# Scaling the softmax probabilities on GpSimd: the reciprocal as a broadcast tensor operand in place of a per-partition scalar

## What is computed

```python
xn = layernorm(x)
q, k, v = per-head projections of xn            # 16 heads, 64 wide, with biases
scores  = q @ k^T / sqrt(64), causal: -inf above the diagonal
att     = softmax(scores, axis=-1) / sqrt(64)
z       = att @ v
attn    = z.reshape(b, s, 16 * 64) @ proj
# feed-forward: base = xn @ W^T; a softmax over 4 experts of the cosine of (xn @ Wp^T + bp) and sim;
# the best expert's weight times its low-rank product (ranks 1, 2, 4, 8)
out = x + attn + base + routed
```

## Time and profile before

| | |
|---|---|
| median of 3 runs | 1488.75 us (1488.54 to 1489.19) |
| profiled execution, its own time | 1484.91 us |
| span of its instructions | 1482.8 us |
| mean granted TensorE clock | 0.998 |
| PE / PEld busy | 1433.1 / 1146.4 us |
| DVE / ACT / POOL busy | 1161.3 / 1057.0 / 1351.0 us |

### The profile page before, as it was taken

The page is one execution under the profiler, slowest core; times in us unless marked ns, Lnnn a source line. Parts: engine busy times, 40 slices in busy tenths (PEclk is TensorE's granted clock), DMA queues, the critical chain, the costliest instruction groups (busy, mean ns, idle before and its releaser), DMA issues. The chain is left out here.

```text
span 1482.8 us, 40863 instructions
## 1 busy us (share of the span) xinstructions
PE 1433.1 (97%) x11036; PEld 1146.4 (77%) x11036; DVE 1161.3 (78%) x4134; ACT 1057.0 (71%) x3032; POOL 1351.0 (91%) x1414
## 2 busy tenths in 40 slices
PE   6999999999999999999999999999999999999998
PEld 5678777777877778778787787878778787777876
DVE  6787878878788787887878778787887878878784
ACT  4777777767777676776777777777777777777774
POOL 5999989999899998999989999998999999999996
PEclk9999999999999999999999999999999999999999
DMA  6444443443444344344443544444444344434431
GB/s 156 106 94 105 101 110 88 103 113 92 105 104 107 90 99 118 88 109 97 107 100 91 123 92 99 104 104 104 91 102 112 92 110 103 107 85 106 108 86 51
DMA packets 112932, 150.65 MB, mean 102 GB/s; under 512 B 18175, under 2 KB 47166, under 8 KB 112830
## 3 DMA queue, kind: packets, MB, share of 16 engines
q1 hardware_dynamic: 112830, 149.68, 42.8%
HBM read 11.20 MB, written 4.19 MB: 10 GB/s over the span
## 5 line engine op out<-in xcount | busy, mean ns | idle before, releaser
L535 POOL TENSOR_SCALAR prob<-prob,rden 128x128 f32<-128x128 f32 (+3 forms) x1024 | 1092.2, 1084 | 81.6 <-DVE rden L798 59.4
L809 DVE CUSTOM_DVE_ANT_0 prob<-scores,mask 128x128 f32<-128x128 f32 (+3 forms) x1024 | 461.6, 485 | 261.3 <-issue 220.1
L613 ACT ACTIVATE prob<-prob,nmax 128x128 f32<-128x128 f32 (+3 forms) x1024 | 564.4, 554 | 102.5 <-DVE nmax L809 99.5
L1060 PE MATMUL ptp<-ident,prob 128*128 128x128 f32 x2560 | 379.3, 275 | 13.7 <-DVE pt L821 9.6
L624 ACT ACTIVATE pt<-ptp 128x128 f32<-128x128 f32 (+3 forms) x512 | 222.1, 434 | 189.7 <-PE ptp L1060 176.5
L1048 PE MATMUL scores<-k_twice,q_parts 128*128 128x128 f32 (+3 forms) x1024 | 332.8, 335 | 17.5 <-DVE nmax L809 9.0
L1084 PE MATMUL zp<-pt,v_sb 128*64 128x64 f32 (+3 forms) x4096 | 335.8, 306 | 0.8 <-DVE z_lo L827 0.8
L1060 PEld LDWEIGHTS ptp<-ident,prob 128*128 128x128 f32 x2560 | 294.8, 140 | 52.0 <-issue 17.6
L1051 PE MATMUL scores<-k_low,q_parts 128*128 128x128 f32 (+3 forms) x1024 | 321.9, 324 | 0.0
L1048 PEld LDWEIGHTS scores<-k_twice,q_parts 128*128 128x128 f32 x1024 | 193.5, 189 | 84.5 <-issue 30.6
L1084 PEld LDWEIGHTS zp<-pt,v_sb 128*64 128x64 f32 x4096 | 210.2, 137 | 53.4 <-issue 43.7
(11 more groups left out here) (141 smaller groups left out, 1703.4 us busy)
## 6 DMA issues: line engine op xcount, KB each, us to landing
k_twice<-k_hi SPq DMA_DIRECT2D x512, 128.0 KB, 2.4
q_parts<-q_hi SPq DMA_DIRECT2D x256, 128.0 KB, 2.4
q_parts<-q_lo SPq DMA_DIRECT2D x256, 128.0 KB, 2.4
xin<-in_L_attn_x_dram SPq DMA_DIRECT2D x16, 256.0 KB, 3.1
xres<-in_L_attn_x_dram SPq DMA_DIRECT2D x16, 256.0 KB, 2.9
out_dram<-osb SPq DMA_DIRECT2D x16, 256.0 KB, 2.5
pt<-in_L_attn_Wq_dram SPq DMA_DIRECT2D x1, 512.0 KB, 4.3
pt<-in_L_attn_Wk_dram SPq DMA_DIRECT2D x1, 512.0 KB, 4.6
```

What stands on the lines that cost most here:

```text
L535: nc.gpsimd.tensor_scalar(part, part, rden[:, s % NROT, h:h + 1], None, ALU.mult)\
L613: nc.scalar.activation(part, part, ACT.Exp, bias=nmax[:, s % NROT, h:h + 1], scale=-1.0, accum_out=den[:, s % NROT, h:h + 1]).then_inc(p_r ...
L809: nc.vector.tensor_tensor_reduce(out=prob[:, s % NROT, h, 0:cols], in0=scores[h][:, 0:cols], in1=mask[:, S - cols:S], scale=-INV_SCALE, sc ...
L1060: done = nc.tensor.transpose(ptp[h][:, P * j:P * j + P], prob[:, s % NROT, h, P * j:P * j + P], ident[:])
```

## The change

In normalise() on POOL, the scaling is no longer a tensor_scalar whose scalar operand is the column rden[:, s % 4, h] (one value per partition), but a tensor_tensor whose second operand is the same column, repeated over width(s) columns by an access pattern with stride zero. Both are in place on prob, in float32, and signal pn_ready as before. The wait for consts_ready and the register step ahead of it (fixed()) go; the wait for r_ready stays. Nothing moves: every engine has the same instructions in the same order, on POOL with tensor_tensor in the 1024 places. The lines behind the change have numbers that are lower by two.

```diff
             def normalise(c, s):
 
-                summed = c.fixed(c.unit(s))
-                pool.wait_ge(consts_ready, 3)
-                pool.wait_ge(r_ready, summed)
+                pool.wait_ge(r_ready, c.unit(s))
                 for h in range(2):
                     part = prob[:, s % NROT, h, 0:width(s)]
-                    nc.gpsimd.tensor_scalar(part, part, rden[:, s % NROT, h:h + 1], None, ALU.mult)\
-                        .then_inc(pn_ready, 1)
+                    scale = rden[:, s % NROT, h:h + 1].to_broadcast([P, width(s)])
+                    nc.gpsimd.tensor_tensor(part, part, scale, ALU.mult).then_inc(pn_ready, 1)
```

## The result

The changed kernel takes 1441.07 us (median of 4 runs, 1440.68 to 1441.54), the kernel before 1488.64 us beside it (4 runs, 1486.26 to 1489.19): a ratio of 0.968, 95% interval 0.967 to 0.970. I had forecast 1464.3 us and a range down to 1452. So the sign was right and the size was a little over half of what came: 47.6 us by the medians, and 43.6 us between the two profiled executions (1484.91 and 1441.31 us), against 24.5 forecast.

What follows compares the result with a forecast made beforehand. TensorE was taken to set the pace. Terms of 9.6 + 10 + 7 + 4.2 = 30.8 us, cut to four fifths, 24.5 us, took the median of 1488.75 to 1464.3 us; range 1452 to 1481.

Steps and rivals of the forecast that it cites:

- The price: POOL's new scaling instruction: 398, 612, 826 and 1040 ns for the four widths, POOL losing 362 us of work.
- (b): Rival on POOL's scaling: new instruction priced like two full operands, 2.33 ns per column, giving 1473 us; chance 0.10.
- (e): Rival on POOL's scaling: second operand makes the instruction twice as dear, POOL the bound, near 2450 us; chance 0.01.
- Term 1: VectorE's wait for POOL's root of the norms, delaying TensorE's scores, goes whole: 0.6 x 16 = 9.6 us.
- Term 2: TensorE's weight loads waiting directly for POOL, 13.2 us in the whole program: 10 us kept as gain.
- Term 3: VectorE's cast at line 903, held up by POOL's subtraction of line 491, comes sooner: 0.5 x 14 = 7 us.
- Rival (a): Holdups stay: the line 903 cast meets POOL's next instruction, line 496, instead; 16 us remain, 1473 us; chance 0.22.
- Term 4: Smaller VectorE holdups, line 894 beside POOL's casts of line 513, with TensorE waiting for nmax: 0.3 x 14 = 4.2 us.
- The sum: All four terms together, 30.8 us, of which four fifths, 24.5 us, were kept because removed waits uncover VectorE's lateness.
- Rival (c): Gain absorbed: VectorE is late at the same matmuls anyway, only 1 to 7 us remain, 1484 us; chance 0.08.
- Rival (d): Slower: POOL holds up VectorE's SBUF instructions at worse moments in steps 22 and 23, 1496 us; chance 0.02.

Runs made afterwards that it cites:

- e6: Kernel before, all scalings still tensor_scalar, but VectorE takes up POOL's root two steps later: 1485.75 us, ratio 1.001 to the kernel before.

## Why the prediction was off

**Bound.** "TensorE therefore sets the pace, and a faster POOL is worth only the places where TensorE loses time" was right as far as it goes, and so was the search by the starts of matmuls. What I drew from it was wrong. In the stretches where POOL comes late, it is POOL that sets the pace, and TensorE's waits there, direct or through VectorE, are shares of one debt.

**The price** of the new instruction, the saving on POOL (362 us forecast, 381 of busy time measured) and its share of 67% were right. Rivals (b) and (e) are ruled out by the rows of line 534. The rule of the Trainium skill's "GPSIMD Engine Reference" (§ 4.1 Engine selection), one input roughly at line rate and two inputs about 2x slower than VectorE, speaks for the removed instruction. The trace has it the other way round: 2.50 ns per column with the scalar per partition, 1.67 with the repeated tensor.

**Term 1** was right in that VectorE's 30.8 us of waits went whole, though with 0.35 us to spare where I had worked out 0.66. It named VectorE's wait as the cost, and e6 shows that this wait alone is worth nothing: the cost was POOL's lateness behind it. It was sized at 0.6 us a batch and measures 0.86; the allowance of 0.1 us "for what queues up behind it" should have been 0.35, since a score and two transposes follow late. Over the 14 batches of the loop that is 12.1 us, where I had 9.6 for the whole program, 8.4 of it in the loop.

**Term 2**, 10 us: 0.27 and the 0.22 of step 16 are 0.50 us a batch, 7.0 us in the loop, and the eight transposes of the first batch and the draining bring 4.6, together 11.6 us. This term was nearly right.

**Term 3** was taken as 0.5 and measures 0.75 us a batch, 10.5 us instead of 7, all that the cast had been lengthened by. Rival (a), that the cast meets the next POOL instruction, did not come: the cast starts at the very end of line 491 and ends 0.11 us after line 496 has begun, not held up by it. With units 18 to 21 alone it fell to 351 ns on average, with the others alone it stayed at 932.

**Term 4** was right in size: 0.29 us a batch against 0.3, and line 892 at 170 to 173 ns. Its reasons were not: TensorE gains at the q projection, which waits for v_sb, and not at nmax, and units 8 to 11 alone bring the same 170 ns and 0.29 us, so it was lateness handed on to the casts of line 513 and not the two scalings just ahead of them.

**The sum.** "I keep four fifths" is the step that failed, and worst in its reason: "each one removed uncovers what is late next, which is VectorE". Nothing was uncovered that TensorE's starts show. The discount took 6.3 us off a sum of 30.8. It is the largest single error and not the only one, since 43.5 were gained: of the missing 19.0 us the discount is a third. The terms in the loop had been taken as 8.4 + 5.6 + 7 + 4.2 = 25.2 us and measure 12.1 + 7.0 + 10.5 + 4.1 = 33.7, so term 1 was 3.7 us short and term 3 3.5. Another 2.0 us in the loop, half of them at k_twice, and 2.3 of the 7.9 us outside it stood in no term. Without the discount the forecast would have been 1458, still outside what came. The reasoning about discounts would have been right for a change that takes waits away one by one: the root's wait alone and the cast alone bring nothing, 0.95 and 0.79 us a batch won and lost again within 4 us. They are given back to POOL, the engine that this change speeds up. A wait that would come back as a wait for POOL must not be discounted in forecasting a faster POOL.

**Rival (c)** had the right observation, waits that come back, and assigned them to VectorE. That is how it is after the change, for the two places that were tried, not before it. **Rival (d)**: collisions did move, but to a place that costs nothing (below).

## What to carry to other kernels

When an engine with spare time overall is late in places, remove its lateness in thought at all places at once, and follow every wait back to it through other engines; do not discount these terms for each other. To learn whether a wait is a cause or a share of another engine's debt, take away the wait alone and compare the two traces by the start of the n-th instruction on the pacing engine: if the time comes back a few microseconds on, the engine named there is the one to speed up. Pad or price POOL by the distance from start to start, not by recorded durations.

## What the runs showed of the hardware

POOL's multiplication by a value per partition costs 2.50 ns per column as a scalar operand and 1.67 as a tensor with a repeated element; two operands that both change from column to column cost 2.33 between the 128 and 512 column rows.

Some of VectorE's small SBUF instructions are held up by POOL's, and the holdup moves when POOL's timing does. After the change the router's line 882 takes it over, in VectorE's groups before (line 884) and after:

```profile
L884 DVE TENSOR_TENSOR lg<-lg,ramp 128x16 f32<-128x16 f32 x16 | 2.5, 158 | 0.0
```

```profile
L882 DVE TENSOR_TENSOR lg<-lg,ramp 128x16 f32<-128x16 f32 x16 | 14.5, 907 | 0.0
```

Its 0.75 us a batch cost TensorE nothing that the starts show. In all 14 loop batches it ends 0.03 us behind one of POOL's scalings, as line 894 ended 0.03 us behind a cast of line 513 before. The Trainium skill's "SBUF — State Buffer" (§ Who interferes with whom) has a rule that fits: a VectorE instruction with two SBUF inputs contends with a POOL instruction that reads SBUF, one in a mode with two ports, which a cast can enter, contends with POOL, and there whoever issues first keeps the shared ports for its whole instruction while the other is blocked. The ends just behind POOL's agree with that; no run here took the ports apart.
